# A fused attention and ternary feed-forward block: the order of every engine's work rewritten in its plan tables

## The chip, the cores and the metric

One core of one Trainium2 chip. The metric is the device time of one execution in microseconds (us), as the median of the runs. Engine names: PE is the TensorE, DVE the VectorE, ACT the ScalarE, POOL the GpSimd, SP the SyncE, whose queue issues every DMA here.

## The reference

For two sequences of 1024 tokens of width 512: attention with 32 query heads in 8 groups (4 query heads, one key head and one value head of 64 to a group), a residual and layer norm, then a feed-forward step with ternary activations and weights, a residual and layer norm.

```python
y = x * rsqrt(mean(x * x) + 1e-6) * rms_w
y = einsum('bsm,cm->bsc', y, w_in)          # q, k, v of all groups
q, k = _rope(q), _rope(k)
qk = einsum('bghsd,bgxpd->bghsp', q, k) * DQK ** (-0.5)
attn = softmax(where(causal, qk, -inf))
o = einsum('bghsp,bgxpd->bghsd', attn, v)
x1 = _layernorm(x + (x + einsum('bsc,mc->bsm', o, w_out)))
ffn = einsum('bsd,od->bso', ternary(x1), ternary(weight) + rram_variation)
out = _layernorm(x1 + ffn)
```

## The kernel before

The kernel runs one pass for each of the 8 head groups (`over_bodies`): a short first plan that prepares the first chunks, an opening pass, six middle passes that are all alike, and a final pass that also holds the feed-forward step. In a pass the queries of sequence b are cut into tiles s = 0 to 7 of 128; tile (b, s) needs s + 1 key blocks, so a pass has 72 units of one key block each. For each unit PE transposes the probabilities of four heads (L1219), ACT and DVE split them into a high and a low half (`prob_hi` L793, `prob_lo` L1090), and PE multiplies them with the values (L1127).

All other work is a list of events between the units. Each event has a kind and a place; five engines run through the same list in the same order, each doing its own share of an event and skipping the kinds that don't concern it. The order is written out by hand in four tables: `FIRST` (L100) as a list, `OPENING` (L111), `MIDDLE` (L140) and `FINAL` (L166) as places in steps, eight steps to a unit, 576 to a pass. `body_plan` (L194) sorts the events by place. Only the order counts: nothing waits for a step as such, an engine goes on as soon as the semaphores of its next event allow. The kinds that matter here:

- `pj`, `sw`, `ro`, `hl` (b, half, c): PE projects a chunk of 512 tokens (L1174), twelve matmuls, and ACT copies it to `flat` (L869). SP moves its half-rows to `swapped` with four DMAs, two where c = 2 (L594). POOL rotates it, three operations (L736, L738, L740). ACT and POOL split it into halves (L879 to L885, L748 to L759). Chunk c = 2 holds keys and values, c = 0 and 1 two query heads each. `vt`: PE transposes the values (L1192).
- `sc`, `ex` (b, s, head): PE scores (L1162), DVE adds the mask and takes the maximum (L997), ACT the exponential (L825).
- `rc` (b, s): DVE inverts the four sums and transposes them (L1008, L1012), SP writes them to a scratch in HBM with four small DMAs (L578). `rs`: SP waits until they have landed and reads them back spread over the partitions (`spread`, L588).
- `on`, `oh`, `op` (b, s): DVE scales the output with `spread` (`o_raw`, L1070), ACT and POOL split it (`o_hi` L893, `o_lo` L766), PE multiplies it with w_out (L1202), DVE adds it to `acc` (L1082). The next `on` waits for this `o_lo`.
- `lw`, `w`, `wo`: SP loads the next group's weights (768 KB, L545) once both `wo` have been made, then ACT and DVE split weights (L850, L1017; L857, L1030).

In a table a row of `SCORES` is (places of `sc`), (places of `ex`), place of `rc`, place of `rs`, for tiles (0,2) to (0,7), (1,0) to (1,7) and the next group's (0,0) and (0,1), there written (2,0) and (2,1). A row of `PROJECT` is a (b, half), with (pj, sw, ro, hl) for c = 2, 0, 1, then `vt`; a middle pass has (1,0), (1,1), (2,0), (2,1). A row of `OUTPUT` holds `on`, `oh`, `op` as lags behind the first step of the tile's last unit, 8 (36 b + s (s + 3) / 2), from the past pass's (1,7) on, which stands 8 steps before the pass. PE's results of `pj`, `vt`, `op` and a few others share a ring of two PSUM banks in the order of the list.

On SP the waits stand in its one queue: at an `rc` for DVE, at an `rs` for the rows' landing, at an `sw` for ACT's copy, at `lw` for `wo`, and nothing behind is issued before.

```python
                        elif e[0] == "rs":
                            ...
                            wait(sp, row_in[n], g, 64 * NT, 64 * (kk // 2 + 1))
                            wait(sp, o_t_done, g, 2 * NT, kk - 1)
                            ...
                        elif e[0] == "sw":
                            n = chunk(*e[1:])
                            wait(sp, flat_done, g, CHUNKS, n + 1)
                            for i in range(4 if e[3] < 2 else 2):
                                ...
                        elif e == ("lw",) and plan is not final:
                            wait(sp, wout_done, g, 2, 2)
```

Of the kernel before, what the change touches and what calls it, by code (L numbers as in the profile page):

```python
# [81 lines left out]
class Plan:  # L82
# [7 lines left out]
    def number(self):  # L90
# [7 lines left out]


FIRST = (  # L100
# [9 lines left out]

OPENING = dict(  # L111
    SCORES=(((0, 0, 7, 8), (16, 4, 12, 15), 35, 61), ((9, 23, 30, 39), (43, 34, 40, 42), 52, 116),
# [11 lines left out]
    PROJECT=((((1, 4, 4, 11), (8, 4, 13, 30), (20, 8, 33, 43)), 10),  # L124
# [4 lines left out]
    SQUARES=(0, 10),  # L129
    NORMS=((3, 8), (8, 12), (13, 27), (35, 39), (42, 55), (93, 117), (138, 143), (143, 161)),  # L130
    NORM_O=(4, 9),
    W_OUT=(12, 41),
    LOAD=163,
    NORM_W=(196, 234),
    W_IN=(284, 295, 309, 318),
    OUTPUT=((23, 101, 263), (16, 21, 47), (19, 41, 59), (60, 58, 73), (48, 52, 85), (42, 57, 94), (30, 50, 85),
     (37, 52, 74), (15, 23, 39), (17, 40, 62), (41, 56, 69), (37, 47, 63), (44, 64, 119), (56, 87, 98), (66, 71, 92),
     (25, 40, 63), (23, 124, -31)))

MIDDLE = dict(  # L140
    SCORES=(((0, 0, 0, 3), (6, 1, 0, 4), 8, 55), ((3, 9, 14, 21), (21, 34, 28, 36), 91, 94),
# [11 lines left out]
    PROJECT=((((52, 84, 72, 94), (110, 118, 132, 152), (161, 128, 185, 194)), 96),  # L153
# [3 lines left out]
    NORM_O=(8, 23),  # L157
    W_OUT=(45, 54),
    LOAD=84,
    NORM_W=(131, 219),  # L160
    W_IN=(255, 261, 295, 295),
    OUTPUT=((15, 14, 49), (31, 45, 63), (32, 54, 60), (73, 75, 97), (51, 68, 85), (41, 49, 94), (44, 75, 97),
     (28, 45, 61), (19, 26, 36), (23, 41, 46), (28, 32, 55), (12, 46, 75), (28, 49, 60), (32, 37, 52), (23, 51, 87),
     (17, 37, 61), (23, 117, 110)))

FINAL = dict(  # L166
    SCORES=(((2, 2, 3, 6), (15, 0, 13, 22), 27, 62), ((10, 13, 16, 23), (33, 29, 34, 33), 43, 75),
# [10 lines left out]
    PROJECT=((((2, 0, 39, 124), (39, 37, 90, 144), (157, 168, 182, 200)), 118),  # L178
     (((187, 215, 232, 264), (223, 255, 251, 288), (289, 276, 312, 313)), 288)),
    NORM_O=(1, 19),  # L180
    W_OUT=(26, 30),
    FFN_IN=((70, 100), (110, 147), (133, 183), (209, 286)),
    OUTPUT=((16, 17, 30), (21, 26, 51), (34, 38, 57), (31, 36, 72), (36, 57, 92), (62, 73, 103), (43, 59, 117),
     (53, 71, 92), (17, 32, 50), (32, 43, 65), (43, 70, 86), (54, 76, 91), (66, 67, 81), (54, 95, 126), (60, 81, 95),
     (33, 44, 59), (23, 17, 55)),
    LAYER=((315, 360, 379, 392, 400, 412, 472), (320, 373, 387, 417, 432, 431, 484),
# [5 lines left out]


def body_plan(opening, last):  # L194
    plan = Plan(BODY + (15 if last else 0), BODY)
    at_pass = OPENING if opening else FINAL if last else MIDDLE

    placed = []

    def put(at, e):  # L200
        placed.append((at, len(placed), e))
# [1083 lines left out]
```

## Time and profile before

| | us |
|---|---|
| median of 3 runs | 1394.53 |
| lowest, highest | 1389.77, 1396.01 |
| profiled execution | 1395.41 |
| its span, first to last instruction | 1393.6 |
| PE busy | 1260.4 (90%) |
| DVE busy | 1128.3 (81%) |
| ACT busy | 1028.9 (74%) |
| POOL busy | 756.4 (54%) |

SP has no busy time in a profile: issuing a DMA isn't counted as busy, so its queue is read from the timeline and from what others wait for. The passes can be told by the weight loads (L545), one to a pass. Opening pass: about 48 to 235 us; middle passes: 235 to 1192 us; final pass: from there on.

### The profile page before, as it was taken

The page shows a single profiled execution, that of the slowest core. Times are in us where ns is not written, and L with a number is a line of the kernel's source. Part 1 is how long each engine was busy: PE and PEld are TensorE (multiplying, and loading weights), DVE is VectorE, ACT ScalarE, POOL GpSimd, SP SyncE. Part 2 cuts the span into 40 slices and gives each one's busy share as a digit, 9 for nine tenths or more (in the row PEclk, how much of TensorE's full clock was granted, in tenths as well). Part 3 has the DMA queues.
Part 4 walks back from the last instruction along what each step waited for, and adds up shares of the span by engine and source line. Part 5 has one row for each costly group of instructions (what it writes and reads, how often), then busy time and mean ns, then how long its engine had stood idle before and what let it go on. Part 6 is the DMA issues. An engine that isn't in the chain of part 4 may idle for free.

```text
span 1393.6 us, 29101 instructions
## 1 busy us (share of the span) xinstructions
PE 1260.4 (90%) x9632; PEld 810.3 (58%) x9632; DVE 1128.3 (81%) x2934; ACT 1028.9 (74%) x2199; POOL 756.4 (54%) x776
## 2 busy tenths in 40 slices
PE   4689899998999989998999989998999989998887
PEld 2356565665665656655666656655666656555565
DVE  4588777877897778978898778977888778888987
ACT  5678668777787768777787868867787777777765
POOL 1356554464545547365544646365554745598556
PEclk9799999999999999999999999999999999999999
DMA  6011111111111111111110111111011111121012
GB/s 206 25 31 52 40 33 33 46 39 43 35 48 35 45 31 38 48 33 49 31 51 25 43 35 43 49 30 51 24 38 49 35 40 44 43 65 32 13 40 94
DMA packets 45174, 62.06 MB, mean 45 GB/s; under 512 B 10464, under 2 KB 27104, under 8 KB 45024
## 3 DMA queue, kind: packets, MB, share of 16 engines
q1 hardware_dynamic: 45024, 60.20, 14.6%
q8 instruction: 77, 1.26, 0.4%
q14 instruction: 73, 0.60, 0.2%
HBM read 34.74 MB, written 4.46 MB: 28 GB/s over the span
## 4 chain that ended last, share of the span: by engine, by line
PE 50%; DMA 12%; DVE 10%; POOL 8%; SPq 7%; issue 7%; ACT 5%; DVEq 0%; POOLq 0%; ACTq 0%
PE x L1174 12%; PE t L1219 11%; PE s L1162 9%; PE ot L1127 8%; PE x L1202 7%; DMA spread<-recip_rows 5%; DVE prob L997 3%; DMA swapped<-flat 3%; SPq L594 3%; DMA recip_rows<-turned 3%; SPq L578 3%; DVE prob_lo L1090 2%; POOL flat L740 2%; POOL swapped L736 2%; POOL flat L738 2%
## 5 line engine op out<-in xcount | busy, mean ns | idle before, releaser
L1090 DVE SCALAR_TENSOR_TENSOR prob_lo<-t,prob_hi 128x512 f16<-128x512 f32 x576 | 393.0, 684 | 56.4 <-ACT prob_hi L793 54.4
L793 ACT ACTIVATE prob_hi<-t 128x512 f16<-128x512 f32 x576 | 338.9, 590 | 134.8 <-PE t L1219 130.3
L825 ACT ACTIVATE prob<-prob,neg_max 128x896 f32<-128x896 f32 (+7 forms) x512 | 392.3, 768 | 34.1 <-DVE neg_max L997 31.1
L1219 PE MATMUL t<-ident,prob 128*128 128x128 f32 x2304 | 358.5, 279 | 28.7 <-DVE prob_lo L1090 24.9
L1162 PE MATMUL s<-k_t,q_t 128*128 128x512 f16 (+3 forms) x1536 | 345.4, 328 | 38.9 <-DVE neg_max L997 23.8
L997 DVE CUSTOM_DVE_ANT_0 prob<-s,mask,neg_kappa 128x512 f32<-128x512 f32 (+3 forms) x512 | 320.4, 643 | 56.9 <-PE s L1162 44.5
L1219 PEld LDWEIGHTS t<-ident,prob 128*128 128x128 f32 x2304 | 266.2, 142 | 125.0 <-DVE prob_lo L1090 37.5
L766 POOL TENSOR_TENSOR o_lo<-o_raw,o_hi 128x256 f16<-128x256 f32 x128 | 86.3, 674 | 300.3 <-ACT o_hi L893 298.5
L1162 PEld LDWEIGHTS s<-k_t,q_t 128*128 128x128 f16 x1536 | 141.1, 98 | 122.9 <-DVE neg_max L997 38.8
L1127 PE MATMUL ot<-prob_hi,v_sb 128*64 128x256 f16 x2304 | 203.8, 277 | 0.0
L736 POOL TENSOR_TENSOR swapped<-swapped,sin_sb 128x512 f32<-128x512 f32 (+1 forms) x93 | 118.9, 1278 | 104.0 <-DMA swapped<-flat 102.6
L997 DVE CUSTOM_DVE_ANT_0 prob<-s,mask,low_max 128x128 f32<-128x128 f32 (+3 forms) x256 | 152.7, 605 | 21.1 <-PE s L1162 20.6
L1174 PE MATMUL x<-yt_hi,win_hi 128*128 128x512 f16 x384 | 149.3, 389 | 20.0 <-DVE acc L1082 10.3
L1127 PE MATMUL ot<-prob_lo,v_sb 128*64 128x256 f16 x1152 | 159.4, 273 | 0.0
L1174 PE MATMUL x<-yt_lo,win_hi 128*128 128x512 f16 x384 | 149.3, 389 | 0.0
L1174 PE MATMUL x<-yt_hi,win_lo 128*128 128x512 f16 x384 | 149.3, 389 | 0.0
L1127 PEld LDWEIGHTS ot<-prob_hi,v_sb 128*64 128x64 f16 x2304 | 114.0, 109 | 53.0 <-issue 38.4
L869 ACT ACTIVATE flat<-x 128x512 f32<-128x512 f32 x96 | 57.2, 596 | 95.2 <-PE x L1174 86.0
L740 POOL TENSOR_TENSOR flat<-flat,swapped 128x512 f32<-128x512 f32 (+1 forms) x93 | 119.6, 1286 | 7.3
L738 POOL TENSOR_TENSOR flat<-flat,cos_sb 128x512 f32<-128x512 f32 (+1 forms) x93 | 119.2, 1281 | 0.0
L1202 PE MATMUL x<-wout_hi,o_hi 128*128 128x512 f16 x256 | 97.3, 380 | 12.4 <-POOL o_lo L766 11.9
L1070 DVE SCALAR_TENSOR_TENSOR o_raw<-ot,spread 128x256 f32<-128x256 f32 x128 | 53.4, 417 | 67.3 <-issue 38.4
(103 smaller groups left out, 1690.2 us busy)
## 6 DMA issues: line engine op xcount, KB each, us to landing
swapped<-flat SPq DMA_DIRECT2D x320, 64.0 KB, 2.0
spread<-recip_rows SPq DMA_DIRECT2D x128, 128.0 KB
recip_rows<-turned SPq DMA_DIRECT2D x512, 0.5 KB
raw<-L_attn_w_in SPq DMA_DIRECT2D x8, 768.0 KB, 4.7
raw<-L_attn_w_out SPq DMA_DIRECT2D x8, 512.0 KB, 3.7
out<-acc SPq DMA_DIRECT2D x16, 256.0 KB, 2.0
acc<-L_attn_x SPq DMA_DIRECT2D x3, 1024.0 KB, 10.3
acc<-L_attn_x SPq DMA_DIRECT2D x4, 256.0 KB, 3.8
```

Of the source, the lines that this page charges most:

```text
L736: pool.tensor_tensor(turned_x, turned_x, sin_sb[rows, q_half(half)], ALU.mult).then_inc(products_done, 1)
L738: pool.tensor_tensor(x, x, cos_sb[rows, q_half(half)], ALU.mult).then_inc(products_done, 1)
L740: pool.tensor_tensor(x, x, turned_x, ALU.add).then_inc(roped, 1)
L793: act.activation(prob_hi[:, u % P_RING, :], t_ps[u % 2][:, :], ACT.Copy, scale=P_SCALE).then_inc(prob_hi_done, 1)
L825: act.activation(row, row, ACT.Exp, bias=neg_max[:, kk % 4, h:h + 1], scale=-1.0, accum_out=total[:, kk % 4, h:h + 1]).then_inc(ex_done, 1)
L997: dve.tensor_tensor_reduce(out=prob_row(s, h)[:, c * BANK:c * BANK + cols], in0=s_ps[:, off:off + cols], in1=mask[:, seen:seen + cols], sc ...
L1090: dve.scalar_tensor_tensor(out=prob_lo[:, u % P_RING, :], in0=t_ps[u % 2][:, :], scalar=P_SCALE, in1=prob_hi[:, u % P_RING, :], op0=ALU.mu ...
L1127: mm = pe.matmul(ot_ps[k % 2][a * DH:(a + 1) * DH, 0:2 * P], values_t, part[:, u % P_RING, a * 2 * P:(a + 1) * 2 * P], start=first, stop=last)
L1162: mm = pe.matmul(s_ps[:, off:off + cols], q_t[:, h, s * P:(s + 1) * P], k_t[:, part, keys:keys + cols], start=(part == 0), stop=(part == 1))
L1174: mm = pe.matmul(bank[:, :], w[:, k, some], y[:, k, at], start=(k == 0 and n == 0), stop=(k == KC - 1 and n == 2))
L1202: mm = pe.matmul(bank[:, :], o[:, c, :], w[:, c, :], start=(c == 0 and n == 0), stop=(c == 1 and n == 2))
L1219: mm = pe.transpose(t_ps[u % 2][:, at:at + P], prob_row(s, h)[:, j * P:(j + 1) * P], ident[:, :])
```

## The change

All four tables are rewritten; every plan keeps exactly the same events as before, and no line outside of the tables is touched. Operations, transfers, tiles and semaphores are the same. The table of the middle passes, which is run six times, stands here whole; `FIRST`, `OPENING` and `FINAL` are replaced in the same way. In `FIRST` SP's share keeps its order.

```diff
...
 MIDDLE = dict(
-    SCORES=(((0, 0, 0, 3), (6, 1, 0, 4), 8, 55), ((3, 9, 14, 21), (21, 34, 28, 36), 91, 94),
-     ((37, 37, 44, 53, 53, 56, 58, 65), (49, 56, 57, 75), 110, 121),
-     ((65, 74, 75, 82, 84, 91, 96, 99), (88, 83, 101, 104), 180, 192),
-     ((114, 120, 129, 133, 143, 146, 152, 155), (155, 144, 156, 156), 190, 201),
-     ((159, 161, 164, 167, 180, 185, 194, 199), (185, 204, 201, 211), 228, 248),
-     ((208, 209, 224, 227), (219, 238, 234, 227), 241, 255), ((233, 238, 244, 247), (257, 257, 283, 257), 296, 304),
-     ((249, 260, 269, 272), (304, 300, 293, 307), 306, 323), ((284, 287, 301, 302), (311, 313, 321, 321), 327, 364),
-     ((324, 325, 332, 334, 335, 340, 344, 352), (335, 342, 352, 355), 405, 410),
-     ((363, 366, 377, 377, 386, 386, 388, 392), (380, 382, 395, 397), 421, 462),
-     ((401, 407, 407, 417, 420, 429, 429, 445), (426, 427, 444, 446), 468, 469),
-     ((448, 449, 455, 459, 469, 469, 476, 486), (463, 468, 498, 495), 507, 515),
-     ((496, 500, 508, 513), (517, 517, 516, 540), 553, 566), ((522, 539, 540, 555), (550, 547, 560, 560), 566, 575)),
-    PROJECT=((((52, 84, 72, 94), (110, 118, 132, 152), (161, 128, 185, 194)), 96),
-     (((189, 200, 200, 225), (222, 205, 261, 264), (246, 209, 266, 307)), 233),
-     (((310, 294, 362, 369), (331, 328, 362, 414), (386, 440, 446, 448)), 379),
-     (((445, 456, 472, 491), (472, 486, 502, 572), (507, 536, 554, 574)), 496)),
-    NORM_O=(8, 23),
-    W_OUT=(45, 54),
-    LOAD=84,
-    NORM_W=(131, 219),
-    W_IN=(255, 261, 295, 295),
-    OUTPUT=((15, 14, 49), (31, 45, 63), (32, 54, 60), (73, 75, 97), (51, 68, 85), (41, 49, 94), (44, 75, 97),
-     (28, 45, 61), (19, 26, 36), (23, 41, 46), (28, 32, 55), (12, 46, 75), (28, 49, 60), (32, 37, 52), (23, 51, 87),
-     (17, 37, 61), (23, 117, 110)))
+    SCORES=(((0, 0, 0, 0), (1, 0, 4, 11), 28, 63), ((11, 13, 17, 24), (38, 25, 30, 42), 71, 77),
+     ((31, 37, 45, 50, 51, 56, 58, 63), (54, 54, 56, 67), 119, 119),
+     ((67, 73, 73, 81, 87, 93, 97, 106), (72, 91, 97, 104), 157, 162),
+     ((111, 114, 131, 135, 142, 145, 152, 155), (141, 145, 154, 157), 161, 172),
+     ((162, 173, 179, 191, 195, 202, 210, 211), (184, 194, 206, 213), 225, 249),
+     ((214, 218, 221, 225), (217, 234, 239, 231), 249, 269), ((232, 239, 242, 245), (259, 274, 250, 254), 295, 307),
+     ((245, 259, 262, 268), (293, 300, 286, 302), 314, 336), ((282, 287, 300, 303), (318, 324, 314, 309), 336, 366),
+     ((318, 326, 333, 335, 341, 342, 347, 353), (331, 337, 354, 355), 382, 395),
+     ((361, 364, 378, 378, 387, 387, 390, 393), (384, 383, 392, 398), 438, 452),
+     ((400, 400, 410, 411, 419, 429, 437, 439), (451, 436, 450, 450), 453, 466),
+     ((444, 450, 456, 461, 474, 478, 487, 488), (461, 469, 495, 499), 518, 518),
+     ((502, 514, 516, 520), (540, 515, 518, 535), 549, 550), ((521, 536, 544, 553), (548, 560, 551, 561), 568, 569)),
+    PROJECT=((((46, 29, 83, 92), (109, 93, 143, 160), (160, 153, 173, 201)), 98),
+     (((187, 169, 223, 225), (220, 213, 237, 276), (242, 239, 272, 302)), 235),
+     (((310, 308, 354, 379), (329, 339, 395, 410), (389, 427, 432, 454)), 384),
+     (((454, 446, 465, 490), (475, 457, 510, 575), (508, 478, 574, 575)), 500)),
+    NORM_O=(12, 24),
+    W_OUT=(44, 45),
+    LOAD=2,
+    NORM_W=(121, 133),
+    W_IN=(245, 262, 292, 299),
+    OUTPUT=((16, 27, 48), (29, 52, 61), (35, 47, 57), (48, 75, 99), (52, 68, 87), (39, 56, 100), (63, 70, 88),
+     (28, 41, 63), (9, 13, 27), (12, 37, 48), (27, 35, 52), (41, 53, 77), (43, 45, 71), (16, 39, 55), (44, 53, 87),
+     (31, 42, 63), (23, 117, 110)))
...
```

Two numbers of the other tables are used below. In `FINAL` the `hl` of chunk (1,1,1) moves from 313 to 321 and the first score that needs it from 346 to 336. In `OPENING` `oh` of (0,7) moves from 303 to 319 and `on` of (1,0) from 305 to 324.

## Rows read from the trace of the kernel before

**Rows 1.** The page's busy shares, and one middle pass as a stretch.
```profile
PE 1260.4 (90%) x9632; PEld 810.3 (58%) x9632; DVE 1128.3 (81%) x2934; ACT 1028.9 (74%) x2199; POOL 756.4 (54%) x776
...
554.00:713.00 159.00, 148.34 (x1172) 95.59 (x1171) 130.75 (x349) 121.62 (x263) 85.22 (x82) 1.00 0.14 40
```

**Rows 2.** Groups by line, 235 to 1192 us: busy, mean ns, idle before, releasers.
```profile
L1070 DVE SCALAR_TENSOR_TENSOR o_raw<-ot,spread 128x256 f32<-128x256 f32 x96 | 40.0, 416 | 46.9 <-issue 31.7 <-DMA spread<-recip_rows 11.7 <-POOL o_lo L766 3.4
```

**Rows 3.** Waits, 235 to 1192 us: who for whom, total us, times, longest.
```profile
PE s L1162 <- DVE neg_max L997: 18.7, 16, 2.5
PE t L1219 <- DVE prob_lo L1090: 14.3, 14, 2.0
...
PE x L1174 <- DVE acc L1082: 10.3, 6, 2.1
PE x L1202 <- POOL o_lo L766: 5.9, 6, 2.1
```

**Rows 4.** Timeline of SP's queue in one middle pass: start, duration, DMAs issued.
```profile
583.17 2.44 SPq L594 DMA_DIRECT2D swapped<-flat  x4
...
607.02 0.56 SPq L588 DMA_DIRECT2D spread<-recip_rows  x1
...
642.03 1.29 SPq L578 DMA_DIRECT2D recip_rows<-turned  x4
645.55 0.56 SPq L588 DMA_DIRECT2D spread<-recip_rows  x1
...
650.69 0.55 SPq L588 DMA_DIRECT2D spread<-recip_rows  x1
```

**Rows 5.** Timeline of DVE, same pass; in brackets idle time before and its releaser.
```profile
593.36 0.42 DVE L1070 SCALAR_TENSOR_TENSOR o_raw<-ot,spread 128x256 f32<-128x256 f32 x1 [1.66 <-POOL o_lo L766]
...
612.32 0.42 DVE L1070 SCALAR_TENSOR_TENSOR o_raw<-ot,spread 128x256 f32<-128x256 f32 x1 [2.52 <-DMA spread<-recip_rows]
...
650.04 0.42 DVE L1070 SCALAR_TENSOR_TENSOR o_raw<-ot,spread 128x256 f32<-128x256 f32 x1 [3.05 <-issue]
...
655.16 0.42 DVE L1070 SCALAR_TENSOR_TENSOR o_raw<-ot,spread 128x256 f32<-128x256 f32 x1 [1.78 <-issue]
```

**Rows 6.** Timeline of PE, same pass.
```profile
593.37 0.38 PE L1202 MATMUL x<-wout_hi,o_hi 128*128 128x512 f16 x1 [2.07 <-POOL o_lo L766]
...
613.46 0.39 PE L1174 MATMUL x<-yt_hi,win_hi 128*128 128x512 f16 x1 [2.03 <-DVE acc L1082]
...
650.84 0.60 PE L1162 MATMUL s<-k_t,q_t 128*128 128x512 f16 x2 [2.04 <-DVE neg_max L997]
...
656.58 0.66 PE L1219 MATMUL t<-ident,prob 128*128 128x128 f32 x4 [1.47 <-DVE prob_lo L1090]
```

**Rows 7.** POOL: timeline, same pass, and its split by line, whole span.
```profile
588.75 1.27 POOL L736 TENSOR_TENSOR swapped<-swapped,sin_sb 128x512 f32<-128x512 f32 x1 [4.96 <-DMA swapped<-flat]
...
L748 POOL TENSOR_TENSOR q_t<-flat,q_t 64x512 f16<-64x512 f32 x62 | 71.9, 1160 | 50.9 <-ACT q_t L880 48.8
```

**Rows 8.** DMA issues (count, KB, median us to landing), and POOL's wait for them.
```profile
swapped<-flat SPq DMA_DIRECT2D x320, 64.0 KB, 2.0
...
POOL swapped L736 <- DMA swapped<-flat: 102.6, 44, 6.7
```

**Rows 9.** SP's weight loads, first and last of six; landing of all loads into raw.
```profile
248.06 0.38 SPq L545 DMA_DIRECT2D raw<-L_attn_w_in  x1
...
1044.82 0.39 SPq L545 DMA_DIRECT2D raw<-L_attn_w_in  x1
...
DMA to landing us min/median/max: 3.7/4.1/6.5
```

**Rows 10.** Waits of PE, 48 to 235 us, then two of 1192 to 1394 us.
```profile
PE t L1219 <- DVE prob_lo L1090: 5.7, 4, 2.8
...
PE x L1202 <- POOL o_lo L766: 3.8, 4, 1.5
PE x L1104 <- DVE acc L918: 3.1, 2, 2.7
```

More of the change, by code:

```diff
@@ L100 @@
 FIRST = (
[9 rows of a table removed]
-OPENING = dict(
-    SCORES=(((0, 0, 7, 8), (16, 4, 12, 15), 35, 61), ((9, 23, 30, 39), (43, 34, 40, 42), 52, 116),
[11 rows of a table removed]
-    PROJECT=((((1, 4, 4, 11), (8, 4, 13, 30), (20, 8, 33, 43)), 10),
[4 rows of a table removed]
[L129 to L138, printed above, removed]
@@ L166 @@
-FINAL = dict(
-    SCORES=(((2, 2, 3, 6), (15, 0, 13, 22), 27, 62), ((10, 13, 16, 23), (33, 29, 34, 33), 43, 75),
[10 rows of a table removed]
[L178 to L186, printed above, removed]
[5 rows of a table removed]
[8 rows of a table added]
@@ new lines @@
+OPENING = dict(
+    SCORES=(((0, 1, 4, 5), (3, 3, 10, 9), 52, 72), ((10, 17, 18, 22), (41, 27, 30, 32), 63, 75),
[11 rows of a table added]
+    PROJECT=((((6, 32, 7, 16), (9, 43, 30, 39), (32, 50, 45, 57)), 20),
[4 rows of a table added]
+    SQUARES=(1, 13),
+    NORMS=((7, 12), (13, 15), (15, 19), (24, 33), (47, 57), (98, 119), (122, 133), (149, 173)),
+    NORM_O=(6, 15),
+    W_OUT=(30, 47),
+    LOAD=159,
+    NORM_W=(216, 228),
+    W_IN=(277, 293, 309, 310),
+    OUTPUT=((23, 101, 263), (26, 54, 62), (36, 41, 57), (49, 55, 75), (34, 64, 93), (77, 83, 98), (48, 64, 85),
+     (52, 57, 94), (13, 39, 54), (36, 52, 68), (60, 70, 83), (64, 67, 79), (49, 81, 116), (78, 93, 107),
+     (56, 65, 102), (23, 40, 68), (23, 124, -31)))
@@ new lines @@
+FINAL = dict(
+    SCORES=(((0, 0, 10, 10), (6, 12, 13, 14), 23, 51), ((13, 18, 18, 28), (14, 34, 25, 35), 51, 54),
[10 rows of a table added]
+    PROJECT=((((12, 10, 31, 121), (37, 75, 69, 125), (149, 152, 150, 194)), 134),
+     (((188, 206, 249, 269), (219, 242, 260, 280), (282, 252, 302, 321)), 271)),
+    NORM_O=(4, 15),
+    W_OUT=(24, 28),
+    FFN_IN=((50, 81), (102, 140), (132, 187), (197, 266)),
+    OUTPUT=((12, 19, 31), (15, 30, 44), (14, 25, 58), (32, 53, 73), (39, 57, 93), (41, 78, 98), (37, 64, 108),
+     (41, 56, 99), (14, 38, 52), (45, 48, 76), (49, 69, 86), (59, 67, 91), (54, 63, 90), (66, 79, 103), (41, 63, 87),
+     (24, 36, 58), (19, 17, 76)),
+    LAYER=((323, 360, 366, 387, 394, 414, 421), (332, 380, 394, 414, 439, 438, 457),
[5 rows of a table added]
```

77 rows, old and new, of tables (FIRST, LAYER, PROJECT, SCORES) are left out of this document.

## The prediction

> **What bounds the kernel now.** I read the page's busy shares first, then one middle pass as a stretch, then the waits of the six middle passes, and last the timelines around the longest of them. The TensorE (PE) is busy 90% of the span, and in a middle pass 148.3 of 159 us [rows 1]. Some 10 us a pass is all that can be won from its idle time, so the question is what ends that idle time. The waits of the middle passes (235 to 1192 us) have four large PE rows: scores behind a maximum 18.7 us, transposes behind prob_lo 14.3, projections behind acc 10.3, output products behind o_lo 5.9 [rows 3]. In three of the four PE waits for the VectorE (DVE), which is itself not full. The reader should ask what DVE was waiting for: in the same stretch it stands idle 46.9 us before one instruction, o_raw (the "on" event), 7.8 us a pass [rows 2]. DVE works in order, so all that follows o_raw stands too.
>
> The timelines show the three places of a pass, each of which has its like in the other middle passes. (a) Tile (0,5): the spread DMA is issued at 607.02, o_raw starts at 612.32 after 2.52 us of idle, and PE's projection has waited 2.03 us. (b) Tiles (1,1) and (1,2): spreads are issued at 645.55 and 650.69, o_raw starts at 650.04 and 655.16 after 3.05 and 1.78 us of idle (the view calls the releaser "issue", but only the spread is 4.5 us old), and PE has waited 2.04 and 1.47 us. (c) Tile (0,3): a swap of four DMAs is issued at 583.17, GpSimd (POOL) waits 4.96 us for it, makes o_lo only behind its rotation, o_raw loses 1.66 us and PE 2.07 [rows 4 to 7]. All three are late DMAs, issued late because SyncE (SP) issues in order and each issue takes time: 2.44 us for a swap's four, 0.55 for a spread, 1.29 for four rows [rows 4].
>
> **What of PE's waits hangs on this.** The acc row (10.3, six waits) is place (a), the o_lo row (5.9, six waits) place (c). Of the 18.7 us the six waits like the one at 650.84 make 13.5, of the 14.3 us the six like the one at 656.58 make 10.3 and two before (a) 1.5 [rows 3, 6]. Sum 41.5 us, 6.9 a pass.
>
> **The change, part by part.** It moves events only; no instruction, byte or buffer is added, so every cost is one of place. I put one step of the plan (an eighth of a unit, 576 to a pass) at 0.277 us: the weight loads of the six middle passes are issued from 248.06 to 1044.82, five periods of 159.35 us [rows 9]. With the rows' durations I follow the SP queue through both tables. Used: projection to the copied chunk 12 steps (an estimate: twelve matmuls, of which the one at 613.46 is the first of such a dozen, with a copy of 0.6 us behind them, 3.3 us in all); swap 8.6 steps to issue and 7.2 to land (2.44 and 2.0 us) [rows 4, 8]; four rows issue and land in 12.6 (642.03 to the spread that waits for them at 645.55); spread 16 (645.55 to 650.04, 4.5 us) [rows 4, 5]; rotation on POOL 3 times 1.27 us, 13.8 steps, and hi/lo split 2 times 1.16 us, 8.4 steps [rows 7].
>
> Place (a) before: rs(0,5) stands at step 192 and its on at 204, 12 steps for a DMA that takes 16. After: 162 and 223. Place (b) before: on SP rc(1,1), step 296, stands behind sw(2,0,2), 294, whose projection is at 310. SP can't get past it before 322, the spread lands at 353, and on(1,1) is at 332. After: sw(2,0,2), 308, stands behind both rc(1,1), 295, and rs(1,1), 307; on(1,1) is at 331, and on(1,2) has moved from 340 to 369. Place (c) before: oh(0,3), 140, stands behind ro(1,0,0), 132, whose swap lands at 138, so o_lo ends at 154 for an on(0,4) at 153. After: oh(0,3), 140, stands ahead of ro(1,0,0), 143. All 6.9 us a pass should go.
>
> What is late next, by the same walk: on(0,4), 151, whose rows now wait on SP behind sw(1,0,0) (projection 109, issues till 130, rows till 142, spread till 158): 7 steps, 1.9 us. o_lo(0,5), which follows ro(1,1,2), 223, and hl(1,1,2), 225, on POOL and ends at 252 for on(0,6) at 244: 8 steps, 2.3 us. on(0,1), 51, with oh(0,0) at 52: 5 steps, 1.4 us. vt(1,1), 235, with its rotation done at 237: 0.5 us. Together 6.1 us a pass at most, nothing at least. I take half, 3.0: for on(1,1) of before the walk gives 353 less 332, 21 steps or 5.8 us, and its row shows 3.05 [rows 5], since work ahead has slipped as well. Net 6.9 less 3.0 is 3.9 a pass, times 6 is 23 us.
>
> The weight load moves from step 84 to 2, where SP stands at it until wout_lo of step 45 is made, some 7 steps later; the rows of tile (0,2), the swap sw(1,0,2) and rs(0,2), 63, are queued behind, and on(0,2) has moved from 113 to 88. The load lands 4.1 us after its issue in the median of these loads, at most 6.5 [rows 9]: step 67 or 75, the spread at 83 or 91, slack 5 steps or 3 too late. I take nothing; the far bound is 0.8 us a pass. The Trainium skill, "DMA: Bandwidth & Descriptors", section "Queues, rings and completion order", says that on each DMA engine the descriptors of SP's one ring are consumed in ring order, which speaks against this part: the small rows can't overtake the load. By that rule the slack is the 5 steps above and not the 11 that rows sent straight away would leave; the sum is the same. The same page, section "Anatomy of one DMA", has a fit of 2.0 us plus bytes over 436e3 (for the GpSimd path), which would give an estimate of 2.3 us for the spread's 128 KB. By it on(0,4) would not be late and the time would be some 6 us lower; this trace shows 4.5 us, and the measurement decides.
>
> The opening: transposes behind prob_lo lose 5.7 us there [rows 10], the larger ones behind late spreads; in the new table every spread lands ahead of its on. o_lo(0,7) ends 8 steps behind on(1,0), 2.3 us, half again: net 5.7 less 1.1 is 4.6, and I take 5 with the output products that wait there too. The work of the first 50 us keeps SP's order (three swaps, two rows, two spreads); I put it at nothing, 2 us either way. The final pass: PE waits 3.8 us for o_lo and 3.1 for acc [rows 10]; after 1330 us POOL's chain of small steps sets the pace, so I take 5 of 6.9. Sum 23 + 5 + 5 = 33 us. The profiled execution took 1395.4 us (span 1393.6), 0.9 above the median 1394.5: 1395.4 less 33 is 1362.
>
> **The rivals.** First: the queue moves from SP to POOL and all 6.1 us of the late places come to PE. Net 0.8 a pass, 5 us, and of opening and final half, 5: 1385. For it: POOL's waits for swaps are 102.6 us already [rows 8], and (1,0,1) and (1,1,0) land 15 and 11 steps after their ro in the new table. Against: what stands behind these ro on POOL is a split with slack.
>
> Second, nothing comes of it: 1393. Of the four rows, 49.2 us, the SP queue leaves 7.7 unexplained [rows 3]; waits of that kind, one engine of a pair a little behind the other, would have to grow by 3.9 us a pass. For it: DVE's in-order work is moved nearly everywhere. Against: pairs of scores that are less than five steps from the next but one are fewer in each table (9, 7, 7 before, 7, 5, 6 after).
>
> Third, slower: the scores of tile (1,0), third head, at step 221, wait for the split of chunk (1,0,1). Its projection has moved from 161 to 160 but the score from 224 to 221; the walk ends at 215, slack 6.3 steps or 1.75 us. All engines come to a stand when it is late, and each us costs a us in all eight passes. From 33 over 8 plus 1.75, 5.9 us of lateness, the gain is gone. POOL's longest wait for a swap is 6.7 us [rows 8]: at that on top, 8 times 4.95 is 40 us, and 6.7 for chunk (1,1,1) of the final pass, which has no slack: 1362 + 47 is 1409. Against: a swap lands in 2.0 us in the median.
>
> **How the numbers follow.** The forecast has 0.62; the move to POOL 0.20, the one without effect 0.10, the slower one 0.08. What a measurement can tell from no change is about 0.5%, 7 us. The low end is all 41.5 us, 5.7 and 6.9 gained with nothing late, and the 2 us of the start: 1339. The high end takes in the move to POOL: 1387, and leaves out the other two, 0.18. Faster by over 0.5% is the forecast and seven tenths of the move to POOL, whose time lies 9 us under the median and whose price is a bound: 0.76. Within 0.5% are its other three tenths and the rival without effect: 0.16. Slower is the third: 0.08.
>
> **What would show it.** DVE's idle time before o_raw in the six middle passes falls from 46.9 us to about 18; PE's acc and o_lo rows nearly vanish and its score row falls to 5; the period of the weight loads falls from 159.35 to about 155.4. If DVE's idle falls so and the period doesn't, the second rival holds; if POOL's rows for o_lo or swaps end PE's waits, the first; a row of PE scores waiting for POOL's q_t, the third. I would be wrong if PE waits for DVE longer at places where nothing on SP is late.

## The result, and the profile after

The changed kernel takes **1313.53 us** (median of 4 runs, 1312.91 to 1314.63) against 1394.55 for the kernel before (with a fourth run beside the three of the table); the ratio is 0.9425, with a 95% interval of 0.9402 to 0.9449. That is 81 us less where 33 were forecast, and 25 us below the low end of the range. The profiled execution took 1313.5 us, its span 1311.7. `FIRST` is one line shorter, so every line number of after is one smaller: o_raw is L1069, the scores L1161, the transposes L1218, w_out's product L1201.

The busy shares and the chain by engine, from the page of after (beside [rows 1]), and below it the chain of before:

```profile
PE 1246.6 (95%) x9632; PEld 807.0 (62%) x9632; DVE 1121.3 (85%) x2934; ACT 1023.6 (78%) x2199; POOL 762.4 (58%) x776
...
PE 75%; DVE 8%; POOL 5%; issue 4%; ACT 4%; DMA 3%; SPq 2%; POOLq 0%; DVEq 0%; ACTq 0%
```
```profile
PE 50%; DMA 12%; DVE 10%; POOL 8%; SPq 7%; issue 7%; ACT 5%; DVEq 0%; POOLq 0%; ACTq 0%
```

The chain that ended last now runs through PE for three quarters of the span, where it was half; DMAs and SP's issues fell from 19% of it to 5%. The six middle passes as one stretch, first of before, then of after (columns: stretch, its length, busy time of PE, PE's weight loads, DVE, ACT and POOL with their instructions, granted clock, DMA share, GB/s):

```profile
235.00:1192.00 957.00, 898.26 (x7042) 577.59 (x7042) 785.36 (x2086) 731.00 (x1571) 512.79 (x487) 0.99 0.14 40
```
```profile
226.00:1122.50 896.50, 887.08 (x7040) 576.87 (x7039) 779.68 (x2085) 724.75 (x1571) 517.02 (x487) 1.00 0.15 42
```

The stretch is 60.5 us shorter. PE's time without work fell from 957.0 less 898.3, 58.7 us, to 9.4: 49.3 us. Its busy time fell by 11.2 although it does the same matmuls. The rest of the 81 us lies ahead and behind: the time up to the stretch fell by 9.0 us (235.0 to 226.0), what follows it by 12.4.

In the same stretch of after, the group of o_raw, the DVE wait that it stands for, and all of PE's waits (engine, line, waited for: total us, times, longest):

```profile
L1069 DVE SCALAR_TENSOR_TENSOR o_raw<-ot,spread 128x256 f32<-128x256 f32 x96 | 40.1, 418 | 6.9 <-DMA spread<-recip_rows 6.5
```
```profile
DVE o_raw L1069 <- DMA spread<-recip_rows: 6.5, 6, 2.3
...
PE s L1161 <- DVE neg_max L996: 4.3, 5, 0.9
...
PE s L1161 <- DVE low_max L996: 1.7, 6, 0.3
PE t L1218 <- DVE prob_lo L1089: 1.6, 4, 0.8
...
PE t L1218 <- ACT prob L824: 0.7, 1, 0.7
PE ot L1126 <- DVE prob_lo L1089: 0.6, 2, 0.4
```

Against [rows 2] DVE's idle time before o_raw fell from 46.9 to 6.9 us, six waits at one place, on(0,4). Against [rows 3] the rows for acc (10.3) and o_lo (5.9) are gone, the score row fell from 18.7 to 4.3 and the transposes from 14.3 to 1.6.

**Place (b) after the change.** SP's queue and DVE in a middle pass (start, duration, instruction):

```profile
603.87 1.25 SPq L577 DMA_DIRECT2D recip_rows<-turned  x4
...
606.00 0.51 SPq L587 DMA_DIRECT2D spread<-recip_rows  x1
...
608.89 1.21 SPq L593 DMA_DIRECT2D swapped<-flat  x2
```
```profile
613.31 0.42 DVE L1069 SCALAR_TENSOR_TENSOR o_raw<-ot,spread 128x256 f32<-128x256 f32 x1
```

Rows and spread of tile (1,1) are issued ahead of the swap, and o_raw has no idle time in front of it, where [rows 5] showed 3.05 us.

**The clock.** In before three stretches of the middle passes show half clock (1.2 GHz), 3.4 us each, behind PE waits of 1.9, 2.1 and 1.3 us at place (a). One of them as a window, another window at full clock (2.4 GHz), and a dozen projection matmuls in the chain of each:

```profile
452.00:456.00 4.00, 4.00 (x12) 1.59 (x11) 1.52 (x5) 0.49 (x2) 3.84 (x5) 0.58 0.06 19
476.00:480.00 4.00, 3.31 (x18) 1.83 (x19) 3.93 (x13) 3.69 (x9) 1.31 (x3) 1.00 0.03 11
```
```profile
451.78 4.45 PE x L1174 x12
...
476.69 2.76 PE x L1174 x12
```

The dozen takes 1.69 us longer; three times that is 5 of the 11.2 us of busy time. Not every such wait has half clock behind it: the middle passes of before hold nineteen PE waits of 1.28 us or more, and the other sixteen, the longest of 2.55 us among them, show none. After shows no such stretch in its middle passes. What the other 6 us of busy time were is open; they are no work, since the matmuls are the same.

### The profile page after: what moved, and what is told of

It is laid out like the page before. It is cut to its first block, busy times and chain, and to the rows that moved or that the text cites. A ratio compares the mean times of both kernels' runs of the same rounds, so it can differ in the third digit from the quotient of the medians.

```text
span 1311.7 us, 29125 instructions
## 1 busy us (share of the span) xinstructions
PE 1246.6 (95%) x9632; PEld 807.0 (62%) x9632; DVE 1121.3 (85%) x2934; ACT 1023.6 (78%) x2199; POOL 762.4 (58%) x776
## 4 chain that ended last, share of the span: by engine, by line
PE 75%; DVE 8%; POOL 5%; issue 4%; ACT 4%; DMA 3%; SPq 2%; POOLq 0%; DVEq 0%; ACTq 0%
PE t L1218 17%; PE x L1173 16%; PE s L1161 16%; PE ot L1126 13%; PE x L1201 11%; DVE prob L996 2%; DVE prob_lo L1089 2%; SPq L593 1%; DMA swapped<-flat 1%; ACT prob L824 1%; DMA spread<-recip_rows 1%; PE x L1110 1%; PE x L1191 1%; POOL inv_std L637 1%; DVE win_lo L1016 1%
## 5 line engine op out<-in xcount | busy, mean ns | idle before, releaser
L1161 PE MATMUL s<-k_t,q_t 128*128 128x512 f16 (+3 forms) x1536 | 350.7, 329 | 23.5 <-DVE neg_max L996 7.3
L1218 PE MATMUL t<-ident,prob 128*128 128x128 f32 x2304 | 355.7, 278 | 5.4 <-DVE prob_lo L1089 4.3
L1218 PEld LDWEIGHTS t<-ident,prob 128*128 128x128 f32 x2304 | 264.4, 141 | 97.3 <-issue 34.8
L1161 PEld LDWEIGHTS s<-k_t,q_t 128*128 128x128 f16 x1536 | 141.5, 99 | 101.9 <-DVE neg_max L996 22.1
L1173 PE MATMUL x<-yt_hi,win_lo 128*128 128x512 f16 x384 | 146.6, 382 | 0.0
L747 POOL TENSOR_TENSOR q_t<-flat,q_t 64x512 f16<-64x512 f32 x62 | 71.6, 1155 | 97.4 <-ACT q_t L879 95.5
L1081 DVE SCALAR_TENSOR_TENSOR acc<-x,out_scale,acc 128x512 f32<-128x512 f32 x128 | 95.3, 744 | 9.7 <-PE x L1201 9.3
```

The lines of the kernel that those rows point to most:

```text
L1161: mm = pe.matmul(s_ps[:, off:off + cols], q_t[:, h, s * P:(s + 1) * P], k_t[:, part, keys:keys + cols], start=(part == 0), stop=(part == 1))
L1173: mm = pe.matmul(bank[:, :], w[:, k, some], y[:, k, at], start=(k == 0 and n == 0), stop=(k == KC - 1 and n == 2))
L1218: mm = pe.transpose(t_ps[u % 2][:, at:at + P], prob_row(s, h)[:, j * P:(j + 1) * P], ident[:, :])
```

## The experiments

All runs stand beside runs of the kernel before on the same chip (medians of 1394 to 1396 us).

**1. The middle table alone**, all else as before, and **2. the other three tables alone**.

> The kernel before with the new MIDDLE table alone; FIRST, OPENING and FINAL stay. By the traces the span from the first output scaling of the first middle pass to that of the final pass fell from 957.2 to 896.6 us. If the tables' shares simply add, this run takes 1394.5 less 61, 1334 us, within 4. If the new passes fit only each other (the last tiles of a pass are worked in the next one), a part is lost at both seams: 1340 or more.

> The kernel before with the new FIRST, OPENING and FINAL, and the old MIDDLE: the complement of middle_only, which took 57.5 us off. If the tables' shares add, the rest is 81 less 57.5, 24 us: 1371 within 4. The prediction allowed 10 us for these tables: 1384.

Measured: 1337.53 us, ratio 0.959 (0.9571 to 0.9608), 57.5 us less; and 1371.38 us, 0.9826 (0.9805 to 0.9846), 24.9 less, two and a half times the 10 us of the prediction. Both lie where adding shares put them, and the shares do add up: 82.4 against 81.

**3. Only the three places**, three numbers of the kernel before moved so that these places have the order of the change: on(0,5) later, sw(2,0,2) behind the rows, oh(0,3) ahead of its rotation.

```diff
-     (((310, 294, 362, 369), (331, 328, 362, 414), (386, 440, 446, 448)), 379),
+     (((310, 324, 362, 369), (331, 328, 362, 414), (386, 440, 446, 448)), 379),
...
-    OUTPUT=((15, 14, 49), (31, 45, 63), (32, 54, 60), (73, 75, 97), (51, 68, 85), (41, 49, 94), (44, 75, 97),
+    OUTPUT=((15, 14, 49), (31, 45, 63), (32, 54, 60), (73, 75, 97), (51, 59, 85), (41, 49, 94), (63, 75, 97),
```

> The kernel before with three events of MIDDLE moved: the output scaling on(0,5) 19 steps later, the swap sw(2,0,2) behind rs(1,2) on SyncE, the split oh(0,3) ahead of the rotation ro(1,0,0). Theory L (the late transfers of the three places are what the kernel before loses in a middle pass): TensorE gets back the 41.5 us of waits counted there and some 5 us of half clock behind them, so 1394.5 less 42 to 47, 1348 to 1353. Rival W (the old table as a whole is too tight; a stall that is taken away comes back at the next tight event): less than 15 us, 1380 or more.

Measured: 1356.37 us, 0.9724 (0.9708 to 0.974): 38.6 us less with three numbers. That is 3 us short of the range of theory L, and far from rival W. The middle passes as a stretch, o_raw, and PE's waits there:

```profile
235.00:1153.00 918.00, 894.87 (x7046) 575.48 (x7045) 785.00 (x2088) 728.02 (x1573) 515.09 (x487) 1.00 0.15 41
```
```profile
L1070 DVE SCALAR_TENSOR_TENSOR o_raw<-ot,spread 128x256 f32<-128x256 f32 x97 | 40.3, 416 | 2.1 <-issue 1.6 <-POOL o_lo L766 0.3
```
```profile
PE t L1219 <- DVE prob_lo L1090: 5.5, 12, 0.8
PE x L1174 <- DVE win_lo L1017: 5.5, 6, 0.9
PE s L1162 <- DVE neg_max L997: 5.4, 11, 0.9
```

DVE's 46.9 us before o_raw are gone but for 2.1, and with them PE's large rows. PE's idle time in the stretch fell from 58.7 to 23.1 us, 35.6, and its busy time by 3.4. What is left to the changed kernel is 21.5 us of stretch: 23.1 less 9.4, 13.7 us of PE's idle time, and 7.8 of its busy time.

**4. The three places undone** in the changed kernel: rows and spreads of tiles (0,5) and (0,6) late, so that the spread of (0,5) again stands 12 steps ahead of its `on`; sw(2,0,2) ahead of the rows of (1,1); oh(0,3) behind the rotation of chunk (1,0,0).

```diff
-     ((67, 73, 73, 81, 87, 93, 97, 106), (72, 91, 97, 104), 157, 162),
-     ((111, 114, 131, 135, 142, 145, 152, 155), (141, 145, 154, 157), 161, 172),
+     ((67, 73, 73, 81, 87, 93, 97, 106), (72, 91, 97, 104), 199, 211),
+     ((111, 114, 131, 135, 142, 145, 152, 155), (141, 145, 154, 157), 200, 212),
...
-     (((310, 308, 354, 379), ...
+     (((310, 294, 354, 379), ...
...
-    OUTPUT=(..., (52, 68, 87), ...
+    OUTPUT=(..., (52, 73, 87), ...
```

> The changed kernel with three events of MIDDLE put back as tight as before: rc(0,5), rc(0,6) and their spreads late, the spread of (0,5) 12 steps ahead of its use; sw(2,0,2) ahead of rc(1,1) on SyncE; oh(0,3) behind ro(1,0,0). Theory L: the 41.5 us and the half clock come back, 1313.5 plus 42 to 47, 1355 to 1360. Rival W: the new table takes up what is late, under 15 us, up to 1328.

Measured: 1354.99 us, 0.971 (0.9676 to 0.9744): 41.5 us more than the changed kernel. Its o_raw stands idle 47.4 us in all, and PE's waits for maxima are back:

```profile
L1069 DVE SCALAR_TENSOR_TENSOR o_raw<-ot,spread 128x256 f32<-128x256 f32 x96 | 40.1, 418 | 47.4 <-issue 26.5 <-POOL o_lo L765 8.1 <-PE ot L1126 7.5
```
```profile
PE s L1161 <- DVE neg_max L996: 24.9, 11, 3.6
PE x L1201 <- POOL o_lo L765: 10.3, 6, 1.7
```

The run is no mirror of run 3, though its 41.5 us are the number that the prediction had counted. Place (b) is back at on(1,1) alone, where six waits of PE make 20.6 us, and place (c), with 10.3 us for o_lo. At place (a) o_raw loses 7.5 us, but behind PE's own products and not behind the spread, and PE has no wait for acc. From 226 to 1166 us PE's idle time is 30.4 us longer than in the changed kernel and its busy time 13.1, with 23.9 us at half clock. That the sum equals 41.5 is luck.

**5. One number of these**, sw(2,0,2) at 294 in the changed kernel, where 308 was behind the rows of tile (1,1).

> The changed kernel with one event of MIDDLE moved: sw(2,0,2) from step 308 to 294, ahead of rc(1,1), where it stood in the old table. SyncE then waits at it for a projection of step 310 while the rows of (1,1) are ready behind it. Theory L: place (b) alone, TensorE loses 3 to 4 us a pass, 18 to 24 us, and some 10 us of half clock behind it: 1331 to 1348. Rival: the new table has put the use of the spread late enough, 1313 to 1318.

Measured: 1344.25 us, 0.9648 (0.9628 to 0.9667), 30.7 us more. SP, DVE and PE in one pass:

```profile
617.35 1.21 SPq L593 DMA_DIRECT2D swapped<-flat  x2
618.67 2.02 SPq L577 DMA_DIRECT2D recip_rows<-turned  x4
...
621.57 0.56 SPq L587 DMA_DIRECT2D spread<-recip_rows  x1
```
```profile
626.45 0.42 DVE L1069 SCALAR_TENSOR_TENSOR o_raw<-ot,spread 128x256 f32<-128x256 f32 x1 [4.59 <-issue]
```
```profile
627.95 1.02 PE L1161 MATMUL s<-k_t,q_t 128*128 128x512 f16 x4 [3.60 <-DVE neg_max L996]
```

The swap goes out first and the rows right behind it; o_raw starts 4.9 us after the spread's issue, DVE has stood for 4.59 us and PE for 3.60. The middle passes as a stretch, and what follows on such a wait of PE (3.48 us, ended at 935.71):

```profile
224.00:1154.00 930.00, 898.69 (x7050) 581.86 (x7047) 782.02 (x2087) 726.05 (x1574) 517.07 (x488) 0.99 0.14 41
...
936.00:941.00 5.00, 5.00 (x37) 3.61 (x36) 3.88 (x10) 3.09 (x8) 2.80 (x3) 0.66 0.29 78
```

Of 33.5 us more than after, 21.9 are idle time of PE and 11.6 busy time: 20.5 us of the middle passes ran at half clock, which is worth about 10 (an estimate: half of them).

**6. The weight load back** at step 84 (LOAD=84 in place of 2).

> The changed kernel with the weight load of the middle passes put back from step 2 to step 84 of SyncE's queue, nothing else. In the changed trace SyncE stands some 10 us a pass at this load. The prediction priced the move at nothing, at most 0.8 us a pass lost: by it this run takes 1313.5 within 4, at best 5 us less. The rival, that the early load was itself a gain (norm and split of the weights are free to start earlier), expects 1320 or more.

Measured: 1313.22 us, 0.942 (0.9401 to 0.9438): no difference from 1313.53. In the changed kernel SP stands at the load for long, and pays nothing for it (the queue's own waits, middle passes):

```profile
SPq L544 <- DVE wout_lo L1029: 57.3, 6, 10.0
```

**7. One of the predicted new holes made real**: o_lo(0,5) eight steps later (lag 70 to 78), behind the rotation of chunk (1,1,0) on POOL.

> The changed kernel with one event of MIDDLE moved: oh(0,5) behind the rotation ro(1,1,0), by 8 steps. The changed trace shows o_lo(0,5) ready only 0.2 us before on(0,6) starts, so that three POOL operations ahead of it (3.8 us) leave on(0,6) some 3.6 us late in each of six passes. Theory J (the new table is just in time and has no slack, each us late costs a us): 1313.5 plus 22, and some us of half clock if TensorE stands long enough, 1335 to 1345. Rival (TensorE has enough work queued to run through it): under 10 us, up to 1323.

Measured: 1336.11 us, 0.9567 (0.9544 to 0.9589), 22.6 us more, and o_raw's group shows what for:

```profile
L1069 DVE SCALAR_TENSOR_TENSOR o_raw<-ot,spread 128x256 f32<-128x256 f32 x97 | 40.5, 418 | 30.0 <-POOL o_lo L765 22.4 <-DMA spread<-recip_rows 6.9 <-PE ot L1126 0.2
```

**8. The other one taken away**: the rows of tile (0,4) at 90 in place of 119, ahead of sw(1,0,0) on SP.

> The changed kernel with rc(0,4) of MIDDLE at step 90 in place of 119, ahead of the swap sw(1,0,0) on SyncE, so that its spread lands before on(0,4). That o_raw is the only one that still waits in the middle passes, 6.9 us in all six. Theory J: up to 6.9 us off, 1307 to 1311 as TensorE's waits are 8.8 us in all. Rival: those waits lie elsewhere, 1313 within 2.

Measured: 1310.67 us (1308.91 to 1311.32), 0.939 (0.9371 to 0.9409), 2.9 us under the changed kernel, the lowest of all kernels here (the intervals of the two ratios overlap at their ends, the runs don't). o_raw's idle time is 0.5 us:

```profile
L1069 DVE SCALAR_TENSOR_TENSOR o_raw<-ot,spread 128x256 f32<-128x256 f32 x97 | 40.4, 416 | 0.5
```

**9. What the other 21 us are.** Five runs put single groups of events in place. First all places of scores and exponentials (`sc`, `ex`) of the new table with the three places only, and those of the old table in the changed kernel.

> The kernel before with the three moved events (three_places, 1356.4 us) and, in MIDDLE, the places of all scores and exponentials taken from the new table; everything else of MIDDLE stays. The three places leave 21 us of the middle passes' gain unexplained (917.8 to 896.6 us in the traces). Theory Q (these are TensorE's small waits behind VectorE's maxima, so the order of the scores holds them): 1336 to 1344. Rival N (no group of events holds them alone; an order fits only as a whole): 1352 or more, and it may well be slower than three_places.

> The changed kernel with the places of all scores and exponentials of MIDDLE taken from the old table; projections, outputs, rows and spreads stay new. Theory Q: the 21 us come back, 1332 to 1338. Rival N: anything above, as the old scores meet events they were not ordered for; if under 1320, the scores have no share in the 21 us.

Measured: 1523.29 us, 1.092 (1.0893 to 1.0947), and 1399.57 us, 1.0043 (1.0029 to 1.0057). Both mixtures are slower than either of their parents, the first by 167 us against 1356.37, the second by 86 against 1313.53 (and 5 us over the kernel before). PE's first waits in the one and the other:

```profile
PE s L1166 <- DVE neg_max L1001: 55.4, 56, 2.5
PE s L1166 <- DVE low_max L1001: 28.8, 30, 2.5
PE t L1223 <- ACT prob L829: 28.5, 12, 5.4
```
```profile
PE s L1165 <- DVE neg_max L1000: 41.2, 40, 2.3
PE s L1165 <- DVE low_max L1000: 18.5, 24, 1.5
```

A mixture brings collisions of its own. In the first one the last exponential of tile (0,2) stands at step 11, but its `rc` at 8, ahead of it, and DVE stands there once in each pass:

```profile
DVE recip L1012 <- ACT prob L829: 20.1, 6, 3.4
```

So these two runs price the mixtures, and not what the scores' places are worth.

Then the wait for win_lo, 5.5 us in the run with three places, by the places of the weight splits: the new ones with the three places (NORM_W 121, 133 and W_IN 245, 262, 292, 299 for 131, 219 and 255, 261, 295, 295); the last two splits earlier (276, 284 for 295, 295); and the old ones in the changed kernel.

> The kernel before with the three moved events of three_places (1356.4 us) and, in MIDDLE, the norm and the split of the next weights at the new places (NORM_W 121, 133; W_IN 245, 262, 292, 299): the last two splits no longer stand back to back on VectorE. In the trace before TensorE waits 5.4 us for them in the middle passes (0.9 a pass). Theory R (what three_places leaves of the gain is many small waits, each paid in full): 5 us off, 1351. Rival: the other engines are behind by as much at that point, 1355 or more.

> The kernel before with the three places moved (as the run three_places, 1356.4 us), and the last two of the four weight splits at steps 276 and 284 in place of 295 and 295. With the three places alone, the first matmul of the projection at step 310 waited six times 0.9 us, 5.5 in all, for the last win_lo of DVE. Theory R, every wait of PE counts in full: the win_lo row goes and the time falls by about 5 us, 1351 (1349 to 1353.5). Rival, the waits that the three places leave only change their place: the win_lo row goes, other PE rows grow by as much, and the time is 1354 to 1360.

> The changed kernel (1313.5 us) with the places of the weight splits and of their scales of the kernel before: NORM_W 131 and 219 for 121 and 133, W_IN 255, 261, 295, 295 for 245, 262, 292, 299. If a projection's wait for win_lo is bound to these places, it comes back, six times 0.9 us, and the time is 1318 to 1321. If it came from the work of DVE around them, it doesn't, and the time is 1311 to 1316.

Measured: 1359.7 us, 0.9741 (0.972 to 0.9762), with the wait still there (5.6 us), so that this edit tells nothing of what the wait is worth. The earlier splits: 1359.35 us, 0.9753 (0.9728 to 0.9778), and the wait is gone, but PE's others grew (230 to 1140 us):

```profile
PE s L1162 <- DVE neg_max L997: 11.6, 19, 0.9
PE t L1219 <- DVE prob_lo L1090: 5.4, 12, 0.5
PE ot L1127 <- DVE prob_lo L1090: 4.9, 12, 0.6
```

The row for maxima went from 5.4 to 11.6 and that of the products with the values from 1.6 to 4.9, and the middle passes are no shorter. The rival holds here: a wait of this kind only changes its place. The old places in the changed kernel: 1330.35 us, 0.9547 (0.9527 to 0.9568), 16.8 more; no wait for win_lo comes back, but two others come that the changed kernel doesn't have:

```profile
PE x L1173 <- DVE acc L1081: 8.9, 6, 1.5
PE x L1191 <- POOL flat L739: 5.1, 6, 1.1
```

Neither of its two expectations was right. So the 21 us have no owner among these groups: taken singly into the kernel with three places, scores and weight splits bring nothing or a loss, and taken singly out of the changed kernel each costs more than the 21 us or nearly all of it. That the new order holds only as a whole would fit this, but isn't shown: the mixtures have collisions of their own, and the places of projections, rows, spreads and outputs beyond the three were not tried alone. How the 21 us divide, and which waits would have to go together, stays open.

## Why the prediction was right and wrong

**The mechanism and its size: right.** Late DMAs on SP's one queue stop DVE at o_raw, and PE behind it. The prediction counted 41.5 us of PE's waits at three places; moving these places alone took 38.6 off, 35.6 of them idle time of PE. Undoing them put 41.5 on, a like number by another sum (run 4). It also holds for one number: a swap fourteen steps too early costs 30.7 us, 20.6 of them in six waits of PE. Places (a) and (c) were moved only together with (b).

**The weight load: right.** Priced at nothing, measured at 0.3 us. The Trainium skill, "DMA: Bandwidth & Descriptors", section "Queues, rings and completion order", has the descriptors of one ring consumed in their order, though a later one may finish its write before an earlier one. The prediction took from it that the small rows can't overtake the load; the two places of the load gave the same time, so no run here shows whether they would have. The 4.1 us that the prediction took for the load's landing are the median of two kinds of loads; the 768 KB load alone took 4.7 us in the median in before. That is two steps more and leaves 3 of the 5 steps of slack; the sum stays as it was.

**"What is late next": wrong, and a third of the error.** This step took 3.0 us a pass, 18 us, off the 41.5. Of its four holes only on(0,4) came, 6.5 us of DVE over six passes, 1.1 a pass for 1.9; taking it away gained 2.9 us (run 8), which is about what it cost. The largest, o_lo(0,5) behind the rotation of chunk (1,1,2), was to be 2.3 us late. POOL and DVE in after show it in time:

```profile
581.40 1.27 POOL L735 TENSOR_TENSOR swapped<-swapped,sin_sb 64x512 f32<-64x512 f32 x1
...
589.11 0.67 POOL L765 TENSOR_TENSOR o_lo<-o_raw,o_hi 128x256 f16<-128x256 f32 x1
```
```profile
584.62 0.42 DVE L1069 SCALAR_TENSOR_TENSOR o_raw<-ot,spread 128x256 f32<-128x256 f32 x1
...
590.04 0.42 DVE L1069 SCALAR_TENSOR_TENSOR o_raw<-ot,spread 128x256 f32<-128x256 f32 x1
```

The rotation and on(0,5) both stand at step 223, but POOL starts the first at 581.40 and DVE the second at 584.62, 3.2 us later. The walk had let no engine begin an event before its step, though nothing waits for a step as such: POOL runs ahead wherever its inputs are there. So o_lo ends at 589.78, 0.26 us before DVE's next o_raw (0.21 in the mean of six passes). Nor is a step 0.277 us everywhere: PE begins the transposes of units 27, 28 and 29, eight steps apart, at

```profile
580.88 0.61 PE L1218 MATMUL t<-ident,prob 128*128 128x128 f32 x4
...
584.14 0.61 PE L1218 MATMUL t<-ident,prob 128*128 128x128 f32 x4
...
585.89 0.66 PE L1218 MATMUL t<-ident,prob 128*128 128x128 f32 x4
```

that is after 3.26 and then 1.75 us. The chain of dependences was right, its times weren't: eight steps on top do make it late, and cost 22.6 us (run 7).

The same part weighed the fit of "DMA: Bandwidth & Descriptors", section "Anatomy of one DMA", of the Trainium skill: by its estimate of 2.3 us for a spread on(0,4) would not have been late. It was late, and from a spread's issue to its use 4.5 us passed [rows 4, 5] and 4.9 (run 5); the measurement decides.

**The bound of the gain: wrong.** The low end, 1339, let only the waits go that were put down to SP. The middle passes with the three places alone take 918 us, the changed ones 896.5: 13.7 us of other waits, of the kind of the second rival, and 7.8 us of PE's busy time went too. The second rival had these waits down as 7.7 us that would have to grow; the four rows it looked at were not all, for PE's idle time in the stretch was 58.7 us and not 49.2, and they shrank. No step of the prediction asked what a better order could do for them, nor counted the half clock behind the long waits as part of the stalls' price (5 us here).

**Opening and final pass: the right sign, too small.** 10 us were taken, 24.9 measured (run 2). The prediction counted the waits of a few rows [rows 10]; by the traces PE's idle time fell by 8 us up to the first middle pass and by 11 in the final pass, and DVE's before o_raw from 11.4 to 0.4 us in the opening and from 9.0 to 0.0 in the final pass. So the same late spreads were likely at work there too; no run moves single places of these tables.

**The rivals.** The move to POOL, 1385: POOL's waits for swaps end no PE wait in the middle passes of after, where PE's row for o_lo is gone. The slower one, 1409: in the middle and final passes no PE score waits for POOL's q_t. In the opening pass two do, which none did in before, for 1.8 us in all:

```profile
PE s L1161 <- POOL q_t L750: 1.8, 2, 1.2
```

The opening became shorter all the same. The signs given: o_raw's idle time was to fall to about 18 us and fell to 6.9; the score row was to fall to 5 and is 4.3; the acc and o_lo rows vanished. The period of the weight loads was to be 155.4 us and is 149.4 (first and last of six, five periods):

```profile
237.66 0.36 SPq L544 DMA_DIRECT2D raw<-L_attn_w_in  x1
...
984.54 0.37 SPq L544 DMA_DIRECT2D raw<-L_attn_w_in  x1
```

The error of 48 us is thus 15 from holes that didn't come, 15 from opening and final pass and some 18 to 21 from the middle order as a whole, less 3 by which the three places fell short of 41.5. Summed again with what the runs gave: 38.6 for the three places, 24.9 for the other tables, and 17 to 21 us of the middle order as a whole make the 81.

## What to carry to other kernels

Where an engine that works in order stands idle in front of one instruction, ask which DMA queue it waits for and what is ahead of that DMA in the queue. Such a stall costs what the bound engine waits for it, and not the idle time of the engine between (run 4: 47.4 us of DVE, 30.4 of PE); half clock can come on top. In a walk through a plan let every engine run ahead as far as its inputs allow: steps that nothing waits for are an order, not a time, and holes found by holding engines to them need not exist. And before two tight orders are mixed to price a part of one, follow the mixture through: it can bring stalls that neither has, and here the gain beyond the named stalls could not be put on any group that was tried.

## What the runs showed of the hardware

In before three PE waits of 1.3 to 2.1 us were followed by 3.4 us at half clock, and sixteen of 1.3 to 2.6 us were not. With one wait of 3.0 to 3.7 us in each of six passes (run 5) half clock showed at four of them, 20.5 us in all, so the length of the wait alone doesn't tell. A queue that stands is no loss by itself: SP stood up to 10.0 us at the weight load without any cost, while one swap in the wrong place, for which SP stood until its chunk was copied and then issued for 1.21 us, cost five us in each pass.
